# The row products of layer 4 in seven slabs: three fp16 products of split parts in place of one fp32 product

## The chip, the cores and the metric

The kernel runs on one core of a Trainium2 chip. The metric is the device time of one execution in microseconds (us). The engines have short names here: PE is TensorE (PEld its weight loads), ACT is ScalarE, DVE is VectorE, POOL is GpSimd, SP issues DMAs.

## The reference, cut to what matters

Four graph layers run one after the other over 4096 nodes with 128 features and a dense 4096 x 4096 matrix `adj`; a residual sum and a layer norm follow each. The change is in the fourth, a gated recurrent cell:

```python
def _L3_gnn_ref(states, adj, W_msg, b_msg, W_ih, W_hh, b_ih, b_hh):
    agg = adj @ states
    msg = relu(agg @ W_msg.T + b_msg)
    gi = msg @ W_ih.T + b_ih          # i_r, i_z, i_n
    gh = states @ W_hh.T + b_hh       # h_r, h_z, h_n
    r = sigmoid(i_r + h_r)
    z = sigmoid(i_z + h_z)
    n = tanh(i_n + r * h_n)
    return (1.0 - z) * n + z * states
x = layernorm(x + _L3_gnn_ref(x, adj, ...))
```

## The kernel before

**Slabs and turns.** A slab is 512 rows of `adj`, so there are eight. In layer 4 (`l == 3` in the code) PE gathers `agg` of a slab, transposed (128 features x 512 rows), in one of the two halves of the PSUM tile `acc`, slab s in half s % 2. A turn (`multiply`) is two blocks of 128 columns of `adj`. Each block takes three fp16 products of 128x512 (L629, L630, L636): both operands were split into a high and a low fp16 part, and high x high, high x low and low x high are summed. So a turn is six products, a slab has 16 turns, and layer 4 has 128. SP loads two turns' data (1 MB) at a time into six places (`group_in`), each as soon as its place is free.

**Row steps.** What follows `agg` in a slab is written as numbered steps k (`rows3` for slabs 0 to 6, `last3` for slab 7). The table `ROWS_FROM[3]` says ahead of which turn step 0 of a slab stands: 30, 43, 56, 69, 82, 96, 112 and 122 for slabs 0 to 7. PE does step k ahead of turn `ROWS_FROM + k` (`hooks`), so its row products are put between the turns. ACT and DVE hold the same steps in the same order of turns; where steps of two slabs fall on one turn, the older slab comes first. Every step waits on the count of all steps of that slab before it, in the order of the list `ROWS[3]`.

**The steps of one slab**, with PE's products in fp32 (`WT` holds the eight transposed weight matrices):

- k=0: PE transposes the slab's states into PSUM `rows_c` ("turn_h", L729).
- k=1: ACT reads `acc` into `turned` (`read_acc`, L918), and `rows_c` into `spare(own+1)` ("h_copy", L997). From then on `acc` is free for slab s+2 (`acc_reads`).
- k=3: PE, "message" (L734); k=4: ACT, relu (L1000).
- k=6, 7: PE, gates r and z, two products each (L737, L738, L741, L742); k=8: PE, "hidden_n" (L745); k=12: PE, "input_n" (L748). That is seven fp32 products in a slab.
- k=8, 10: ACT, two tanh and a bias (L1003, L1006, L1008); k=13: DVE, "r_times" and "n_in" (L1668, L1671); k=14: ACT, tanh ("n_act", L1011); k=16, 17: DVE, "h_minus_n", "z_times", "h_new" (L1674, L1677, L1680).
- k=19 to 25: PE turns the result back (L752), DVE adds x and gathers the norm's statistics, POOL takes the power, ACT scales (L949) and issues the DMA of the output.

Of the kernel before, what the change touches and what calls it, by code (L numbers as in the profile page):

```python
# [7 lines left out]
F16 = mybir.dt.float16  # L8
# [4 lines left out]
P = 128  # L13
# [28 lines left out]
Y0_LOW = 2048.0  # L42
Y_SCALE = 256.0
WHOLE = A_SCALE * Y_SCALE

# [29 lines left out]
for at, s in enumerate(ORDER[1]):  # L75
    ROWS_FROM[1][s] = ENDS1[at] if at != 1 else ENDS1[at] + 1
    if at >= 2:
# [41 lines left out]
    ["turn_h", "h_copy", "message", "message_act", "gate_r", "gate_z", "hidden_n", "r_act", "z_act", "hidden_bias",  # L119
     "input_n", "r_times", "n_in", "n_act", "h_minus_n", "z_times", "h_new", "turn_new", "combine"] + LN,  # L120
]

# [18 lines left out]
def build(nc, x, adj, w0, w1, b1, alpha, beta, w_msg, b_msg, w_ih, w_hh, b_ih, b_hh, out, scratch, dis_out):  # L141
    with ExitStack() as ctx:
# [61 lines left out]
        def kept_slot(n):  # L204
            return parts[:, 2 * UNIT * n:2 * UNIT * (n + 1)].rearrange("p (b z w) -> p b z w", z=2, w=SLAB)

        ident = sb("ident", [P, P])
        WT = sb("WT", [P, 8, P])
        bias1 = sb("bias1", [P, D])
# [15 lines left out]
        peak = sb("peak", [P, 4, 4])  # L225
        row_peak = sb("row_peak", [P, 4])
        neg_peak = sb("neg_peak", [P, 4])
        exp_sum = sb("exp_sum", [P, 4, 2])
        row_sum = sb("row_sum", [P, 2])
        inv_sum = sb("inv_sum", [P, 2])  # L230
# [28 lines left out]

        tile_in = [sem(f"tile_in{c}") for c in range(GROUPS)]  # L260
        turned_up = sem("turned_up")
        high_done = sem("high_done")
        low_done = sem("low_done")
        low_by_turns = sem("low_by_turns")
# [58 lines left out]
        def row_before(l, s, name):  # L323
            return row_base(l, s) + ROWS[l].index(name)

        acc_reads = [2, 1, 1, 1]
        acc_base = [sum(acc_reads[i] * SLABS for i in range(l)) for l in range(4)]

        def acc_reads_done(l, s):
            return acc_base[l] + (place_in(l, s) + 1) * acc_reads[l]  # L330

        def part_free(b):
            return product_base[2] + max(b - 3, 0)
# [204 lines left out]
        def _(pe):  # L538
# [170 lines left out]
            def rows2(k, s):  # L709
                if k == 8:  # L710
# [4 lines left out]
                        last = pe.transpose(acc[:, s % 2, mine], t_of[s % 2][:, q, :], ident[:])  # L715
                    last.then_inc(row[s % 2], 1)

            def rows3(k, s):
                par = s % 2
                own = 6 * par  # L720
                rows_a, rows_b, rows_c = rows_of[par]
                if k == 0:
                    pe.wait_ge(row[par], row_before(3, s, "turn_h"))
                    if s < 2:
                        pe.wait_ge(scores_read, 16 * SLABS)
                        pe.wait_ge(mixed_done, NB * SLABS)
                    pe.wait_ge(x_back[s], 16)
                    for q in range(Q):
                        last = pe.transpose(rows_c[:, P * q:P * (q + 1)], x_nat[:, Q * s + q, :], ident[:])  # L729
                    last.then_inc(row[par], 1)  # L730
                if k == 3:
                    pe.wait_ge(row[par], row_before(3, s, "message"))
                    pe.wait_ge(acc_read, acc_reads_done(3, s))
                    pe.matmul(rows_a, WT[:, 1, :], turned[par][:], start=True, stop=True).then_inc(row[par], 1)  # L734
                if k == 6:
                    pe.wait_ge(row[par], row_before(3, s, "gate_r"))
                    pe.matmul(rows_b, WT[:, 2, :], spare(own + 0), start=True, stop=False)  # L737
                    pe.matmul(rows_b, WT[:, 5, :], spare(own + 1), start=False, stop=True).then_inc(row[par], 1)  # L738
                if k == 7:
                    pe.wait_ge(row[par], row_before(3, s, "gate_z"))  # L740
                    pe.matmul(rows_c, WT[:, 3, :], spare(own + 0), start=True, stop=False)  # L741
                    pe.matmul(rows_c, WT[:, 6, :], spare(own + 1), start=False, stop=True).then_inc(row[par], 1)  # L742
                if k == 8:
                    pe.wait_ge(row[par], row_before(3, s, "hidden_n"))
                    pe.matmul(rows_a, WT[:, 7, :], spare(own + 1), start=True, stop=True).then_inc(row[par], 1)  # L745
                if k == 12:
                    pe.wait_ge(row[par], row_before(3, s, "input_n"))
                    pe.matmul(rows_b, WT[:, 4, :], spare(own + 0), start=True, stop=True).then_inc(row[par], 1)  # L748
# [91 lines left out]
        def _(act):  # L840
# [149 lines left out]
            def rows3(k, s):  # L990
                par = s % 2
                own = 6 * par
                rows_a, rows_b, rows_c = rows_of[par]
                if k == 1:
                    read_acc(3, s)
                    act.wait_ge(row[par], row_before(3, s, "h_copy"))
                    act.activation(spare(own + 1), rows_c, ACT.Copy).then_inc(row[par], 1)  # L997
                if k == 4:
                    act.wait_ge(row[par], row_before(3, s, "message_act"))
                    act.activation(spare(own + 0), rows_a, ACT.Relu, bias=gate_bias[:, 0:1]).then_inc(row[par], 1)  # L1000
                if k == 8:
                    act.wait_ge(row[par], row_before(3, s, "r_act"))
                    act.activation(spare(own + 2), rows_b, ACT.Tanh, scale=0.5, bias=half_bias[:, 0:1]).then_inc(row[par], 1)  # L1003
                if k == 10:
                    act.wait_ge(row[par], row_before(3, s, "z_act"))
                    act.activation(spare(own + 3), rows_c, ACT.Tanh, scale=0.5, bias=half_bias[:, 1:2]).then_inc(row[par], 1)  # L1006
                    act.wait_ge(row[par], row_before(3, s, "hidden_bias"))
                    act.activation(spare(own + 4), rows_a, ACT.Identity, scale=0.5, bias=half_bias[:, 2:3]).then_inc(row[par], 1)  # L1008
# [86 lines left out]
            for n in range(TURNS3):  # L1095
                if n < PAIRS // 2:
                    for k in range(3 * n, 3 * n + 3):
                        rows2(k, SLABS - 1)
                if n == 2:
                    y_high(3, SLABS - 2)  # L1100
                if n == PAIRS + 2:
                    y_high(3, SLABS - 1)
                for k, s in hooks(3, n - ACT_LEAD):
                    if s == SLABS - 1:
                        last3(k)
                    else:
                        rows3(k, s)
# [191 lines left out]
        def _(dve):  # L1299
# [74 lines left out]
            dve.tensor_scalar(scal[:, 6:7], scal[:, 4:5], -1.0 / Y_SCALE, None, ALU.mult)  # L1374
            dve.tensor_scalar(scal[:, 7:8], scal[:, 4:5], A_SCALE, None, ALU.mult)
            dve.tensor_scalar(scal[:, 5:6], scal[:, 1:2], 1.0 / XN_SCALE ** 2, None, ALU.mult)
            dve.tensor_copy(half_bias[:, 2:3], gate_bias[:, 6:7])
            link(dve.tensor_tensor(half_bias[:, 0:2], gate_bias[:, 1:3], gate_bias[:, 4:6], ALU.add))
            link(dve.tensor_scalar(half_bias[:], half_bias[:], 0.5, None, ALU.mult))
# [278 lines left out]
            def rows3(k, s):  # L1658
# [4 lines left out]

                def before(name):
                    dve.wait_ge(row[par], row_before(3, s, name))
                if k == 13:
                    before("r_times")
                    dve.scalar_tensor_tensor(spare(own + 2), spare(own + 2), 1.0, spare(own + 4), ALU.add,  # L1668
                                             ALU.mult).then_inc(row[par], 1)
                    before("n_in")  # L1670
                    dve.tensor_tensor(spare(own + 2), rows_b, spare(own + 2), ALU.add).then_inc(row[par], 1)  # L1671
# [176 lines left out]
```

## Time and profile before

| what | value |
|---|---|
| median of 3 runs | 1311.12 us (1306.46 to 1311.75) |
| the profiled execution: its time | 1309.65 us |
| the profiled execution: its span, first to last instruction | 1307.9 us |
| PE busy over the span | 1227.0 us (94%) |
| DVE, ACT, POOL busy over the span | 770.7 us (59%), 685.3 us (52%), 460.1 us (35%) |
| chain that ended last: share of PE | 78% |
| mean granted TensorE clock | 0.987 |

The time is 1.75 us above the span: what lies ahead of the first and behind the last instruction. Shares of the whole span are averages over four layers with different limits, so the part on layer 4 has to be read in layer 4's own stretch, which begins at about 1070 us; its rows steps run from 1112 us on. Matmuls are pipelined: a row's duration is longer than the distance to the next start, and it is the distance between starts that a product costs in a stream.

### The profile page before, as it was taken

The page shows a single profiled execution, that of the slowest core. Times are in us where ns is not written, and L with a number is a line of the kernel's source. Part 1 is how long each engine was busy: PE and PEld are TensorE (multiplying, and loading weights), DVE is VectorE, ACT ScalarE, POOL GpSimd, SP SyncE. Part 2 cuts the span into 40 slices and gives each one's busy share as a digit, 9 for nine tenths or more (in the row PEclk, how much of TensorE's full clock was granted, in tenths as well). Part 3 has the DMA queues.
Part 4 walks back from the last instruction along what each step waited for, and adds up shares of the span by engine and source line. Part 5 has one row for each costly group of instructions (what it writes and reads, how often), then busy time and mean ns, then how long its engine had stood idle before and what let it go on. Part 6 is the DMA issues. An engine that isn't in the chain of part 4 may idle for free.

```text
span 1307.9 us, 20934 instructions
## 1 busy us (share of the span) xinstructions
PE 1227.0 (94%) x7980; PEld 789.5 (60%) x7980; DVE 770.7 (59%) x1769; ACT 685.3 (52%) x995; POOL 460.1 (35%) x433
## 2 busy tenths in 40 slices
PE   5889999999999989869999999999999889999996
PEld 4888888887884544425555656555655544444442
DVE  6856665655643352687787878787878860122213
ACT  6555555555442222168778787878787530123222
POOL 4012231222123232325566665657565560000000
PEclk9899999999999999979999999999999999999998
DMA  9999999999978979466777777877776849978870
GB/s 304 358 416 415 406 397 377 386 350 357 352 288 320 387 299 353 177 241 247 269 265 274 258 268 267 285 268 287 269 278 213 302 178 365 390 272 315 312 267 24
DMA packets 113524, 394.20 MB, mean 301 GB/s; under 512 B 9872, under 2 KB 23440, under 8 KB 91536
## 3 DMA queue, kind: packets, MB, share of 16 engines
q1 hardware_dynamic: 105232, 388.80, 79.7%
q10 hardware_dynamic: 8192, 4.06, 1.1%
q8 instruction: 63, 1.03, 0.3%
q14 instruction: 37, 0.30, 0.1%
HBM read 319.95 MB, written 72.88 MB: 300 GB/s over the span
## 4 chain that ended last, share of the span: by engine, by line
PE 78%; DVE 8%; ACT 5%; DMA 4%; issue 4%; POOL 2%; POOLq 0%; SPq 0%; ACTq 0%; DVEq 0%
PE strip_b L688 8%; PE acc L629 6%; PE acc L630 6%; PE acc L636 6%; PE acc L707 4%; PE acc L705 4%; PE acc L704 4%; PE acc L703 4%; PE acc L605 4%; PE mid L605 4%; PE strip_b L580 3%; PE strip_a L580 3%; PE acc L603 2%; PE mid L603 2%; PE strip_a L671 2%
## 5 line engine op out<-in xcount | busy, mean ns | idle before, releaser
L1224 POOL TENSOR_TENSOR parts<-arena,parts 128x512 f16<-128x512 f32 x237 | 275.6, 1172 | 196.3 <-ACT parts L980 192.4
L980 ACT ACTIVATE parts<-arena 128x512 f16<-128x512 f32 x256 | 158.5, 624 | 111.1 <-DVE arena L1635 102.6
L1635 DVE SCALAR_TENSOR_TENSOR arena<-parts,dis,strip_b 128x512 f32<-128x512 f16 x256 | 188.9, 743 | 29.7 <-PE strip_b L688 22.5
L629 PE MATMUL acc<-arena,Y 128*128 128x512 f16 x428 | 162.8, 380 | 3.5 <-DMA arena<-adj_t 2.0
L688 PEld LDWEIGHTS strip_b<-ident,arena 128*128 128x128 f32 x1024 | 128.2, 142 | 60.9 <-DVE arena L1626 5.4
L688 PE MATMUL strip_b<-ident,arena 128*128 128x128 f32 x1024 | 155.4, 275 | 8.8 <-ACT arena L975 5.7
L630 PE MATMUL acc<-arena,Y 128*128 128x512 f16 x428 | 162.6, 380 | 0.0
L636 PE MATMUL acc<-arena,Y 128*128 128x512 f16 x428 | 162.5, 380 | 0.0
L969 ACT ACTIVATE arena<-arena,neg_peak 128x2048 f32<-128x2048 f32 x64 | 127.3, 1989 | 5.2 <-DVE neg_peak L1605 5.2
L1201 POOL TENSOR_TENSOR sc<-sc,power 128x4 f32<-128x4 f32 x31 | 31.5, 1016 | 279.6 <-DVE sc L1454 279.6
L975 ACT ACTIVATE arena<-arena,weight 128x2048 f32<-128x2048 f32 x57 | 113.4, 1989 | 2.6 <-DVE weight L1619 2.6
L1594 DVE CUSTOM_DVE_ANT_0 arena<-strip_a,arena,scal 128x1024 f32<-128x1024 f32 x64 | 82.0, 1281 | 49.8 <-PE strip_a L673 32.9
L707 PE MATMUL acc<-parts,Y 128*128 128x512 f16 x256 | 97.1, 379 | 3.4 <-POOL parts L1224 3.4
L703 PE MATMUL acc<-parts,Y 128*128 128x512 f16 x256 | 97.0, 379 | 0.1
L704 PE MATMUL acc<-parts,Y 128*128 128x512 f16 x256 | 97.0, 379 | 0.0
L705 PE MATMUL acc<-parts,Y 128*128 128x512 f16 x256 | 97.0, 379 | 0.0
L1594 DVE CUSTOM_DVE_ANT_0 arena<-mid,arena,scal 128x1024 f32<-128x1024 f32 x58 | 74.3, 1282 | 34.7 <-PE mid L673 34.7
L580 PE MATMUL strip_a<-ident,arena 128*128 128x128 f32 x512 | 67.7, 276 | 13.6 <-DVE parts L1422 10.3
L629 PEld LDWEIGHTS acc<-arena,Y 128*128 128x128 f16 x428 | 42.0, 98 | 57.4 <-issue 11.4
L630 PEld LDWEIGHTS acc<-arena,Y 128*128 128x128 f16 x428 | 42.0, 98 | 55.8 <-issue 13.1
L1668 DVE SCALAR_TENSOR_TENSOR arena<-arena 128x512 f32<-128x512 f32 x7 | 4.8, 692 | 117.4 <-PE mid L748 87.8
L605 PE MATMUL acc<-Y,parts 128*128 128x260 f16 (+1 forms) x286 | 72.8, 291 | 0.0
(332 smaller groups left out, 2559.1 us busy)
## 6 DMA issues: line engine op xcount, KB each, us to landing
arena<-adj_t SPq DMA_DIRECT2D x107, 1024.0 KB, 6.0
arena<-in_adj SPq DMA_DIRECT2D x64, 1024.0 KB, 9.5
arena<-in_adj SPq DMA_DIRECT2D x128, 512.0 KB, 5.8
parts<-adj_t SPq DMA_DIRECT2D x128, 512.0 KB, 7.3
adj_t<-parts SPq DMA_DIRECT2D x37, 1024.0 KB, 8.2
adj_t<-arena SPq DMA_DIRECT2D x27, 1024.0 KB, 9.2
scratch<-v ACTq DMA_DIRECT2D x8, 256.0 KB, 10.6
arena<-scratch SPq DMA_DIRECT2D x8, 256.0 KB, 4.6
```

Of the source, the lines that this page charges most:

```text
L605: last = pe.matmul(acc0[q][:, 0:width], high, Y[:, j, 0:width], start=False, stop=stop)
L629: pe.matmul(to, y_high, high, start=j == 2 * FIRST[l][s], stop=False)
L630: pe.matmul(to, y_low, high, start=False, stop=False)
L636: last = pe.matmul(to, y_high, low, start=False, stop=j == NB - 1)
L688: last = pe.transpose(strip_b[:, b % 2, P * q:P * (q + 1)], unit_in[:, place, P * (j % 8):P * (j % 8 + 1)], ident[:])
L703: pe.matmul(to, Y[:, j, YD:YD + D], kept_slot(b // 2 % KEPT_SLOTS)[:, b % 2, 1, :], start=j == 0, stop=False)
L704: pe.matmul(to, Y[:, j, 0:D], part_h[:, b % 4, :], start=False, stop=False)
L707: pe.matmul(to, Y[:, j, 0:D], part_l[:, b % 4, :], start=False, stop=j == NB - 1).then_inc(product, 1)
L980: act.activation(part_h[:, b % 4, :], mixed[b % G_SLOTS], ACT.Copy).then_inc(high_done, 1)
L1224: pool.tensor_tensor(part_l[:, b % 4, :], mixed[b % G_SLOTS], part_h[:, b % 4, :], ALU.subtract).then_inc(low_done, 1)
L1594: dve.tensor_tensor_reduce(unit_in[:, place, :], flat(scores_at(i)[:]), unit_in[:, place, :], scal[:, 5:6], NEG_HUGE, ALU.mult, ALU.max, p ...
L1635: dve.scalar_tensor_tensor(mixed[b % G_SLOTS], kept_slot(n % KEPT_SLOTS)[:, b % 2, 0, :], dis[:, j:j + 1], strip_b[:, b % 2, :], ALU.mult, ...
```

## The change

Every fp32 operand of the seven row products of slabs 0 to 6 is now held as a high and a low fp16 part, scaled by 16 (rows) or 256 (weights), and each product is three fp16 products. Slab 7 stays as it was. ACT writes the high part, DVE the low part (the value less its high part). The weights are split once, at the start of layer 4. `acc` is now read twice per slab (by ACT and by DVE) before it is free. The scale is undone in the ACT and DVE instructions that read the results.

```diff
+        w_high = parts[:, 12 * UNIT:12 * UNIT + 7 * P].rearrange("p (n w) -> p n w", w=P)
+        w_low = parts[:, 14 * UNIT:14 * UNIT + 7 * P].rearrange("p (n w) -> p n w", w=P)
...
-        acc_reads = [2, 1, 1, 1]
+        acc_reads = [2, 1, 1, 2]
...
+            def three(to, w, held, start, stop):
+                pe.matmul(to, w_high[:, w - 1, :], held[:, 0, :], start=start, stop=False)
+                pe.matmul(to, w_low[:, w - 1, :], held[:, 0, :], start=False, stop=False)
+                return pe.matmul(to, w_high[:, w - 1, :], held[:, 1, :], start=False, stop=stop)
...
                     pe.wait_ge(acc_read, acc_reads_done(3, s))
-                    pe.matmul(rows_a, WT[:, 1, :], turned[par][:], start=True, stop=True).then_inc(row[par], 1)
+                    if s == 0:
+                        pe.wait_ge(w_low_up, 1)
+                    three(rows_a, 1, split_row(turned[par][:]), True, True).then_inc(row[par], 1)
...
-                    pe.matmul(rows_b, WT[:, 2, :], spare(own + 0), start=True, stop=False)
-                    pe.matmul(rows_b, WT[:, 5, :], spare(own + 1), start=False, stop=True).then_inc(row[par], 1)
+                    three(rows_b, 2, split_row(spare(own + 0)), True, False)
+                    three(rows_b, 5, split_row(spare(own + 5)), False, True).then_inc(row[par], 1)
...
                 if k == 1:
-                    read_acc(3, s)
+                    act.wait_ge(product, slab_product(3, s))
+                    act.activation(split_row(turned[par][:])[:, 0, :], acc[:, par, :], ACT.Copy,
+                                   scale=ROW_SCALE / WHOLE).then_inc(acc_read, 1)
                     act.wait_ge(row[par], row_before(3, s, "h_copy"))
                     act.activation(spare(own + 1), rows_c, ACT.Copy).then_inc(row[par], 1)
+                    act.wait_ge(row[par], row_before(3, s, "h_high"))
+                    act.activation(split_row(spare(own + 5))[:, 0, :], rows_c, ACT.Copy, scale=ROW_SCALE).then_inc(row[par], 1)
                 if k == 4:
+                    act.wait_ge(row[par], row_before(3, s, "message_high"))
+                    act.activation(split_row(spare(own + 0))[:, 0, :], rows_a, ACT.Relu, scale=ROW_SCALE / ROWS3,
+                                   bias=msg_bias[:]).then_inc(row[par], 1)
                     act.wait_ge(row[par], row_before(3, s, "message_act"))
-                    act.activation(spare(own + 0), rows_a, ACT.Relu, bias=gate_bias[:, 0:1]).then_inc(row[par], 1)
+                    act.activation(spare(own + 2), rows_a, ACT.Relu, scale=ROW_SCALE / ROWS3,
+                                   bias=msg_bias[:]).then_inc(row[par], 1)
...
+                if n == 4:
+                    act.wait_ge(product, product_base[3])
+                    act.activation(w_high, WT[:, 1:8, :], ACT.Copy, scale=W_SCALE).then_inc(w_high_up, 1)
...
+                if k == 2:
+                    held = split_row(turned[par][:])
+                    dve.wait_ge(acc_read, acc_reads_done(3, s) - 1)
+                    dve.scalar_tensor_tensor(held[:, 1, :], acc[:, par, :], ROW_SCALE / WHOLE, held[:, 0, :], ALU.mult,
+                                             ALU.subtract).then_inc(acc_read, 1)
+                    before("h_low")
+                    held = split_row(spare(own + 5))
+                    dve.scalar_tensor_tensor(held[:, 1, :], rows_c, ROW_SCALE, held[:, 0, :], ALU.mult,
+                                             ALU.subtract).then_inc(row[par], 1)
+                if k == 5:
+                    before("message_low")
+                    held = split_row(spare(own + 0))
+                    dve.tensor_tensor(held[:, 1, :], spare(own + 2), held[:, 0, :], ALU.subtract).then_inc(row[par], 1)
...
+                if n == PAIRS // 2:
+                    dve.wait_ge(w_high_up, 1)
+                    dve.scalar_tensor_tensor(w_low, WT[:, 1:8, :], W_SCALE, w_high, ALU.mult,
+                                             ALU.subtract).then_inc(w_low_up, 1)
```

The other products, `z`, `hidden_n` and `input_n`, change as gate r does. "n_in" becomes one instruction that also scales.

Three places show where the new instructions stand. The first is PE at the message of slab 1 (`strip_a` is that slab's `rows_a`), before:

```order
L636 MATMUL acc<-arena,Y 128x512
L734 MATMUL strip_a<-turned,WT 128x512 [waits acc_read,row1]
L629 MATMUL acc<-arena,Y 128x512 [waits group_in5]
L630 MATMUL acc<-arena,Y 128x512
L636 MATMUL acc<-arena,Y 128x512
```

The same place in the changed kernel, where L643, L644 and L650 are the products of a turn and L733 to L735 are `three`:

```order
L650 MATMUL acc<-arena,Y 128x512
L733 MATMUL strip_a<-turned,parts 128x512 [waits acc_read,row1]
L734 MATMUL strip_a<-turned,parts 128x512
L735 MATMUL strip_a<-turned,parts 128x512
L643 MATMUL acc<-arena,Y 128x512 [waits group_in5]
L644 MATMUL acc<-arena,Y 128x512
L650 MATMUL acc<-arena,Y 128x512
```

One row became three at the same place among the turns, with the same two waits ahead of it. The second place is ACT from "n_act" of slab 0 (`row0`) to the relu of slab 1 (`row1`), before:

```order
L1011 ACTIVATE arena<-arena,gate_bias 128x512 [waits row0]
L918 ACTIVATE turned<-acc 128x512 [waits product]
L997 ACTIVATE arena<-strip_b 128x512 [waits row1]
L1000 ACTIVATE arena<-strip_a,gate_bias 128x512 [waits row1]
L1003 ACTIVATE arena<-strip_a,half_bias 128x512 [waits row1]
```

And in the changed kernel:

```order
L1043 ACTIVATE arena<-arena,gate_bias 128x512 [waits row0]
L1017 ACTIVATE turned<-acc 128x512 [waits product]
L1020 ACTIVATE arena<-strip_b 128x512 [waits row1]
L1022 ACTIVATE arena<-strip_b 128x512 [waits row1]
L1025 ACTIVATE arena<-strip_a,msg_bias 128x512 [waits row1]
L1028 ACTIVATE arena<-strip_a,msg_bias 128x512 [waits row1]
L1032 ACTIVATE arena<-strip_a,half_bias 128x512 [waits row1]
```

ACT has one instruction more ahead of the message ("h_high", L1022) and one more behind it (two relus, L1025 and L1028). The third place is DVE from "r_times" of slab 0 to its "combine", before:

```order
L1668 SCALAR_TENSOR_TENSOR arena<-arena 128x512 [waits row0]
L1671 TENSOR_TENSOR arena<-mid,arena 128x512 [waits row0]
L1674 TENSOR_TENSOR arena<-arena 128x512 [waits row0]
L1677 SCALAR_TENSOR_TENSOR arena<-arena 128x512 [waits row0]
L1680 SCALAR_TENSOR_TENSOR arena<-arena 128x512 [waits row0]
L1684 TENSOR_TENSOR t<-mid,arena 128x512 [waits row0]
```

And in the changed kernel:

```order
L1717 SCALAR_TENSOR_TENSOR arena<-arena 128x512 [waits row0]
L1720 SCALAR_TENSOR_TENSOR arena<-mid,arena 128x512 [waits row0]
L1705 SCALAR_TENSOR_TENSOR turned<-acc,turned 128x512 [waits acc_read]
L1709 SCALAR_TENSOR_TENSOR arena<-strip_b,arena 128x512 [waits row1]
L1724 TENSOR_TENSOR arena<-arena 128x512 [waits row0]
L1727 SCALAR_TENSOR_TENSOR arena<-arena 128x512 [waits row0]
L1730 SCALAR_TENSOR_TENSOR arena<-arena 128x512 [waits row0]
L1714 TENSOR_TENSOR arena<-arena 128x512 [waits row1]
L1734 TENSOR_TENSOR t<-mid,arena 128x512 [waits row0]
```

The low parts of slab 1's `agg` and states (L1705, L1709) now stand between slab 0's "n_in" and "h_minus_n", and the low part of slab 1's message (L1714) between slab 0's "h_new" and "combine".

## Rows read from the trace of the kernel before

**Rows 1.** The page's first line.

```profile
span 1307.9 us, 20934 instructions
```

**Rows 2.** Busy time by engine, granted clock, DMA share and GB/s, from 1112 us.

```profile
1112.00:1290.00 178.00, 178.00 (x750) 83.44 (x748) 37.88 (x101) 41.91 (x75) 6.06 (x6) 1.00 0.77 287
```

**Rows 3.** PE's waits from 1090 us to the end: total, times, longest.

```profile
PE strip_a L784 <- DVE arena L1720: 4.4, 1, 4.4
PE strip_a L775 <- ACT turned L918: 0.7, 1, 0.7
...
PE acc L629 <- DMA arena<-adj_t: 0.3, 1, 0.3
```

**Rows 4.** PE's timeline in slab 0's rows: start, duration, instruction.

```profile
1116.50 1.02 PE L734 MATMUL mid<-turned,WT 128*128 128x512 f32 x2
1117.36 0.38 PE L629 MATMUL acc<-arena,Y 128*128 128x512 f16 x1
...
1121.25 1.02 PE L737 MATMUL mid<-arena,WT 128*128 128x512 f32 x2
1122.11 1.02 PE L738 MATMUL mid<-arena,WT 128*128 128x512 f32 x2
1122.96 0.38 PE L629 MATMUL acc<-arena,Y 128*128 128x512 f16 x1
```

**Rows 5.** PE's groups, 1112 to 1283 us: count, busy, mean ns, idle before.

```profile
L741 PE MATMUL strip_b<-arena,WT 128*128 128x512 f32 x14 | 7.1, 592 | 0.0
```

**Rows 6.** PE's weight loads, grouped, 1112 to 1290 us.

```profile
L629 PEld LDWEIGHTS acc<-arena,Y 128*128 128x128 f16 x196 | 19.2, 98 | 26.7 <-issue 9.1
```

**Rows 7.** PE's timeline from slab 0's "input_n" to slab 1's first gate.

```profile
1133.31 1.02 PE L748 MATMUL mid<-arena,WT 128*128 128x512 f32 x2
...
1135.46 0.60 PE L729 MATMUL strip_b<-ident,arena 128*128 128x128 f32 x4
...
1139.78 1.02 PE L734 MATMUL strip_a<-turned,WT 128*128 128x512 f32 x2
...
1144.96 1.02 PE L737 MATMUL strip_a<-arena,WT 128*128 128x512 f32 x2
```

**Rows 8.** ACT's timeline in the same stretch.

```profile
1135.82 0.72 ACT L1011 ACTIVATE arena<-arena,gate_bias 128x512 f32<-128x512 f32 x1 [5.36 <-DVE arena L1671]
1136.44 0.58 ACT L918 ACTIVATE turned<-acc 128x512 f32<-128x512 f32 x1
1136.92 0.59 ACT L997 ACTIVATE arena<-strip_b 128x512 f32<-128x512 f32 x1
1140.84 0.69 ACT L1000 ACTIVATE arena<-strip_a,gate_bias 128x512 f32<-128x512 f32 x1 [3.33 <-PE strip_a L734]
```

**Rows 9.** DVE's timeline in the same stretch.

```profile
1134.37 0.69 DVE L1668 SCALAR_TENSOR_TENSOR arena<-arena 128x512 f32<-128x512 f32 x1 [54.36 <-PE mid L748]
1135.09 0.69 DVE L1671 TENSOR_TENSOR arena<-mid,arena 128x512 f32<-128x512 f32 x1
1136.57 0.69 DVE L1674 TENSOR_TENSOR arena<-arena 128x512 f32<-128x512 f32 x1 [0.79 <-ACT arena L1011]
1137.30 0.69 DVE L1677 SCALAR_TENSOR_TENSOR arena<-arena 128x512 f32<-128x512 f32 x1
1138.03 0.69 DVE L1680 SCALAR_TENSOR_TENSOR arena<-arena 128x512 f32<-128x512 f32 x1
```

**Rows 10.** Groups that split into high and low parts in other layers.

```profile
L892 ACT ACTIVATE parts<-strip_a 128x1024 f16<-128x1024 f32 x37 | 37.8, 1021 | 33.8 <-PE strip_a L580 33.8
...
L1422 DVE SCALAR_TENSOR_TENSOR parts<-strip_a,parts 128x1024 f16<-128x1024 f32 x37 | 45.2, 1221 | 23.3 <-ACT parts L892 23.3
...
L1640 DVE TENSOR_TENSOR parts<-arena,parts 128x512 f16<-128x512 f32 x19 | 16.0, 840 | 3.9 <-ACT parts L980 3.7
```

**Rows 11.** ACT's timeline at the start of layer 4.

```profile
1085.39 0.63 ACT L882 ACTIVATE Y<-arena 128x512 f16<-128x512 f32 x1 [13.66 <-DMA arena<-scratch]
```

**Rows 12.** Busy time, granted clock, DMA share and GB/s, 1100 to 1120 us.

```profile
1100.00:1120.00 20.00, 19.69 (x92) 9.01 (x91) 0.00 (x0) 1.77 (x3) 0.00 (x0) 1.00 1.01 422
```

More of the change, by code:

```diff
@@ L44 @@
 WHOLE = A_SCALE * Y_SCALE
+ROW_SCALE = 16.0
+W_SCALE = 256.0
+ROWS3 = ROW_SCALE * W_SCALE
 AHEAD = 2
@@ L118 @@
     ["x_sum", "x_scale", "turn_back", "combine"] + LN,
-    ["turn_h", "h_copy", "message", "message_act", "gate_r", "gate_z", "hidden_n", "r_act", "z_act", "hidden_bias",
+    ["turn_h", "h_copy", "h_high", "h_low", "message", "message_high", "message_act", "message_low", "gate_r", "gate_z",
+     "hidden_n", "r_act", "z_act", "hidden_bias",
      "input_n", "r_times", "n_in", "n_act", "h_minus_n", "z_times", "h_new", "turn_new", "combine"] + LN,
@@ L205, in kept_slot, with split_row @@
             return parts[:, 2 * UNIT * n:2 * UNIT * (n + 1)].rearrange("p (b z w) -> p b z w", z=2, w=SLAB)
+        w_high = parts[:, 12 * UNIT:12 * UNIT + 7 * P].rearrange("p (n w) -> p n w", w=P)
+        w_low = parts[:, 14 * UNIT:14 * UNIT + 7 * P].rearrange("p (n w) -> p n w", w=P)
+        def split_row(held):
+            return held.bitcast(F16).rearrange("p (z w) -> p z w", z=2)
         ident = sb("ident", [P, P])
@@ L227, in build @@
         neg_peak = sb("neg_peak", [P, 4])
+        msg_bias = sb("msg_bias", [P, 1])
         exp_sum = sb("exp_sum", [P, 4, 2])
@@ L261, in build @@
         turned_up = sem("turned_up")
+        w_high_up = sem("w_high_up")
+        w_low_up = sem("w_low_up")
         high_done = sem("high_done")
@@ L324, in row_before @@
             return row_base(l, s) + ROWS[l].index(name)
-        acc_reads = [2, 1, 1, 1]
+        acc_reads = [2, 1, 1, 2]
         acc_base = [sum(acc_reads[i] * SLABS for i in range(l)) for l in range(4)]
         def acc_reads_done(l, s):
-            return acc_base[l] + (place_in(l, s) + 1) * acc_reads[l]
+            return acc_base[l] + (place_in(l, s) + 1) * acc_reads[l] - (l == 3 and s == SLABS - 1)
         def part_free(b):
@@ L733, in rows3 @@
                     pe.wait_ge(acc_read, acc_reads_done(3, s))
-                    pe.matmul(rows_a, WT[:, 1, :], turned[par][:], start=True, stop=True).then_inc(row[par], 1)
+                    if s == 0:
+                        pe.wait_ge(w_low_up, 1)
+                    three(rows_a, 1, split_row(turned[par][:]), True, True).then_inc(row[par], 1)
                 if k == 6:
                     pe.wait_ge(row[par], row_before(3, s, "gate_r"))
-                    pe.matmul(rows_b, WT[:, 2, :], spare(own + 0), start=True, stop=False)
-                    pe.matmul(rows_b, WT[:, 5, :], spare(own + 1), start=False, stop=True).then_inc(row[par], 1)
+                    three(rows_b, 2, split_row(spare(own + 0)), True, False)
+                    three(rows_b, 5, split_row(spare(own + 5)), False, True).then_inc(row[par], 1)
                 if k == 7:
                     pe.wait_ge(row[par], row_before(3, s, "gate_z"))
-                    pe.matmul(rows_c, WT[:, 3, :], spare(own + 0), start=True, stop=False)
-                    pe.matmul(rows_c, WT[:, 6, :], spare(own + 1), start=False, stop=True).then_inc(row[par], 1)
+                    three(rows_c, 3, split_row(spare(own + 0)), True, False)
+                    three(rows_c, 6, split_row(spare(own + 5)), False, True).then_inc(row[par], 1)
                 if k == 8:
                     pe.wait_ge(row[par], row_before(3, s, "hidden_n"))
-                    pe.matmul(rows_a, WT[:, 7, :], spare(own + 1), start=True, stop=True).then_inc(row[par], 1)
+                    three(rows_a, 7, split_row(spare(own + 5)), True, True).then_inc(row[par], 1)
                 if k == 12:
                     pe.wait_ge(row[par], row_before(3, s, "input_n"))
-                    pe.matmul(rows_b, WT[:, 4, :], spare(own + 0), start=True, stop=True).then_inc(row[par], 1)
+                    three(rows_b, 4, split_row(spare(own + 0)), True, True).then_inc(row[par], 1)
                 if k == 19:
@@ L1001, in rows3 @@
                 if k == 8:
                     act.wait_ge(row[par], row_before(3, s, "r_act"))
-                    act.activation(spare(own + 2), rows_b, ACT.Tanh, scale=0.5, bias=half_bias[:, 0:1]).then_inc(row[par], 1)
+                    act.activation(spare(own + 2), rows_b, ACT.Tanh, scale=0.5 / ROWS3,
+                                   bias=half_bias[:, 0:1]).then_inc(row[par], 1)
                 if k == 10:
                     act.wait_ge(row[par], row_before(3, s, "z_act"))
-                    act.activation(spare(own + 3), rows_c, ACT.Tanh, scale=0.5, bias=half_bias[:, 1:2]).then_inc(row[par], 1)
+                    act.activation(spare(own + 3), rows_c, ACT.Tanh, scale=0.5 / ROWS3,
+                                   bias=half_bias[:, 1:2]).then_inc(row[par], 1)
@@ L1007, in rows3 @@
                     act.wait_ge(row[par], row_before(3, s, "hidden_bias"))
-                    act.activation(spare(own + 4), rows_a, ACT.Identity, scale=0.5, bias=half_bias[:, 2:3]).then_inc(row[par], 1)
+                    act.activation(spare(own + 4), rows_a, ACT.Identity, scale=0.5 / ROWS3,
+                                   bias=half_bias[:, 2:3]).then_inc(row[par], 1)
                 if k == 14:
@@ L1376, in _ @@
             dve.tensor_scalar(scal[:, 5:6], scal[:, 1:2], 1.0 / XN_SCALE ** 2, None, ALU.mult)
+            dve.tensor_scalar(msg_bias[:], gate_bias[:, 0:1], ROW_SCALE, None, ALU.mult)
             dve.tensor_copy(half_bias[:, 2:3], gate_bias[:, 6:7])
@@ L1670, in rows3 @@
                     before("n_in")
-                    dve.tensor_tensor(spare(own + 2), rows_b, spare(own + 2), ALU.add).then_inc(row[par], 1)
+                    dve.scalar_tensor_tensor(spare(own + 2), rows_b, 1.0 / ROWS3, spare(own + 2), ALU.mult,
+                                             ALU.add).then_inc(row[par], 1)
                 if k == 16:
```

## The prediction

> **What bounds the kernel now.** I read the span first [rows 1]: 1307.9 us, 1.75 us under the profiled execution's time of 1309.65 us. Shares over the whole span say nothing about a change in layer 4, so next come the windows from the first row step to the last turn. From 1112 to 1290 us PE is busy for all 178.00 us, at a granted clock of 1.00, which is the upper of its two levels (2.4 GHz); DVE works 37.88 us of it, ACT 41.91 us, and the DMA engines 0.77 of the time [rows 2]. Then PE's waits, for a full engine may still be one that waits in small bits: from 1090 us on there are three of note, 0.3 us for a load and, in the tail, 0.7 us and 4.4 us for ACT and DVE [rows 3]. The load's wait and the others lie outside the 178 us. So in this stretch PE's own work sets the pace: what leaves PE's stream shortens the time one for one, and work added to ACT or DVE costs nothing as long as PE never has to wait for it. The two questions are therefore the price of a product on PE, and the deadlines that the new splits have to meet.
>
> **The price of a product.** A row's duration is longer than its place in the stream, so I take distances between starts [rows 4]. The two fp32 products of gate r start at 1121.25 and 1122.11, and the next turn's product at 1122.96: 1.71 us for two, 0.855 us each. Between 1117.36 and 1121.25 stand 18 fp16 products of the same 512 columns: 3.89 / 18 = 0.216 us each. Each of these has a weight load of its own, 98 ns long [rows 6], and the pitch shows that it is hidden. Three fp16 products then take 0.648 us, and one replaced product saves 0.855 - 0.648 = 0.207 us.
>
> How many are replaced: an fp32 product leaves two records, and one line of the seven has 14 of them [rows 5], which is one product in each of seven slabs. Seven lines make 49 products (the other lines have 14 records too, some split over two banks). PE loses 49 x 0.207 = 10.1 us.
>
> **What is added beside it, and its deadlines.** The tightest place is the message of slabs 1 to 4, which stand 13 turns apart, so that ACT and DVE still finish the slab before. I follow slab 1 from the start of its transposes on PE, 1135.46, to its message, 1139.78: 4.32 us, three turns and the transposes [rows 7]. Neither moves, since no replaced product stands between them. (Slab 0's "input_n" ends 0.21 us earlier against its start, but the transposes move up with it, and so does what waits for it.)
>
> - ACT in this order: slab 0's tanh at +0.36 us, the read of `acc` at +0.98, the copy of the states from +1.46 to +2.05 [rows 8]. These stay. New behind them is "h_high", which waits on the copy's count; an instruction that waits on the one before it on its own engine starts 0.04 us after its end (1137.30 after 1136.57 + 0.69) [rows 9]. A copy of this shape takes 0.59 us [rows 8], so "h_high" ends at +2.68.
> - DVE: the low part of `agg` waits on the read of `acc` (ended at +1.56) and is done before that. "h_low" starts when "h_high" has ended, and takes 0.69 us like the other 512-column instructions [rows 9]: it ends at +3.41. With 0.05 us to PE the message could start at +3.46. It is wanted at +4.32: 0.86 us to spare.
> - The bounds of these two instructions are the same split in layer 1: at twice the width 1021 ns on ACT and 1221 ns on DVE [rows 10], so at least half of that, 0.51 and 0.61. Upwards I take the relu with its bias from memory, 0.69 us [rows 8], and the slowest subtraction of high parts, 840 ns [rows 10]. With both upper ends the message could start at +3.71, still 0.6 us early. In the middle I keep 0.59 and 0.69, since those rows have the very shape.
>
> The message's own split comes next. ACT's relu starts 1.06 us after the start of the message on PE (1140.84 against 1139.78), that is 0.205 us after its place in the stream; with the shorter product it starts at 0.85 us, and ends at 1.54. The second relu ends at 2.27 us, DVE's subtraction at 3.0 us (3.15 us with 840 ns). Ahead of it in DVE's queue are "h_minus_n", "z_times" and "h_new" of slab 0, now behind "h_low": three times 0.73 us from +3.41, so free at +5.6, which is 1.3 us after the message's start. The first gate is wanted 5.18 us after the message's start now and 4.97 us then [rows 7]: 1.8 us or more to spare. "h_new" itself, late by 1.6 us behind "h_low" [rows 9], is wanted by the transposes just ahead of that gate, more than 3 us later.
>
> `acc` is held longer: slab 2 takes over slab 0's half two turns and the transposes (about 3.0 us) after slab 0's row steps begin; ACT sees PE's end 0.2 us later and reads for 0.58 us, so DVE's read starts by +0.9 and ends by +1.8 us (840 ns). The other slabs have five turns or more.
>
> The split of the weights (896 columns, about 1 us on each engine by the rows of twice this width) stands where ACT is idle for 13.66 us [rows 11] and DVE for 54.36 us [rows 9], and its result is wanted 40 us later. All this costs nothing. Were the cover gone, a wait of x at the message would come back once a slab: 7x in all.
>
> **What could take the gain back.** The loads must keep up with a faster PE. In this stretch they move 287 GB/s [rows 2]; the same bytes in 168 us are 304 GB/s, and the queue has shown 422 GB/s [rows 12]. Only the first 20 us are close: the loads are still catching up there, at full rate, after the 0.3 us wait [rows 3]. PE takes 1 MB in 12 products, 2.59 us, or 405 GB/s, which is under 422, and every row product only widens this. I take nothing off.
>
> The tail, 1290 us to the end, belongs to slab 7, whose products are unchanged, and moves up as a whole.
>
> **Sum.** 1309.65 - 10.1 = 1299.5 us for an execution like the profiled one. That one lies 1.5 us under the median of the runs shown; from the median it would be 1301.0 us. I say 1300 us.
>
> **Rivals.**
>
> *The message waits for its split (7 in 100).* If hand-overs between ACT and DVE take longer than these rows show, PE waits at the message, in seven slabs. It starts to cost when "h_low" is 0.86 us later than worked out. At 1.6 us later half the gain is gone (7 x 0.73 = 5.1 us): 1304.6 us. For it: two instructions on two engines now stand one behind the other in a window that was just long enough for one copy and its margin. Against it: each row in the chain has been seen at its length, and upper ends leave 0.6 us.
>
> *The weight loads of the fp16 products are not hidden (3 in 100).* This ends on the other side. There are 147 fp16 products, and 98 ns each [rows 6] would add 14.4 us: 1309.65 - 10.1 + 14.4 = 1313.9 us, slower than before. It decides from 69 ns on (10.1 / 147), that is, when two thirds of a load show. Against it stands the pitch of 0.216 us in a stream whose stationary operand changes with each product [rows 4]; for it only that the new weights lie in another buffer. The Trainium skill speaks for this rival: "TensorE: Matmul & The Clock Gate", in Part 3 under what overlaps and what doesn't, says that a weight load overlaps matmuls in flight only when its row group differs, and these loads take all rows. By that rule the sum would be 1313.9 us; this trace doesn't agree, with 98 ns of load inside 216 ns of pitch.
>
> *The loads become the bound (5 in 100).* In the first turns PE's gain would turn into a wait for DMA. At most slab 0's part is lost, 7 x 0.207 = 1.4 us: 1301 us. The DMA share of 0.77 speaks against more.
>
> *Something else of PE's order costs as much as it saves (3 in 100):* about 1310 us. No row speaks for it.
>
> **How the numbers follow.** The forecast has 82 in 100. A measurement of this kernel can tell about 0.5%, 6.6 us, from no change. The forecast and the loads as bound lie beyond it (87 in 100); the late message (5.1 us gained), the visible weight loads (4.3 us lost) and part of the last case lie within it (11); 2 are left for slower. The range begins under the lowest run shown less the saving (1306.46 - 10.1 = 1296.4), at 1295.5, and reaches up to the late message, at 1305.
>
> **What the changed profile would show.** Right: 49 threes of fp16 products whose starts are 0.216 us apart, and 0.65 us from the first to the turn's next product; PE busy without a gap from slab 0's rows to the last turn, about 168 us; "h_low" ended 0.6 to 0.9 us ahead of the message of slabs 1 to 4; a span near 1297.8 us. Wrong: PE's waits list the message behind DVE's writing of the states or the gates behind the message's low part; starts of the fp16 threes more than 0.25 us apart; waits for loads after 1112 us; or a granted clock under 1.00 in this stretch.

## The result and the profile after

The changed kernel took 1299.01 us (median of 4 runs, 1297.1 to 1299.96) against 1309.95 us of the kernel before in the same runs (1306.46 to 1311.75). The ratio on record is 0.9922 (the two medians alone give 0.9916), with a 95% interval of 0.9908 to 0.9936: 8.4 to 12.1 us faster. The forecast was 1300 us.

The page of the changed kernel begins with its span:

```profile
span 1296.8 us, 21070 instructions
```

It is 11.1 us shorter than [rows 1]. Not all of this is the change. ACT's first read of `acc` in layer 4 came at 1112.38 us before and at 1111.83 us after, 0.55 us earlier, though ahead of it only the split of the weights was added, in idle time; the ten profiled executions of this study put that read between 1110.0 and 1114.3 us. So the stretch from this read (slab 0) to the same read of slab 7 is the better measure of layer 4. ACT's timeline shows the two reads before:

```profile
1112.38 0.60 ACT L918 ACTIVATE turned<-acc 128x512 f32<-128x512 f32 x1 [26.36 <-PE acc L636]
...
1290.05 0.60 ACT L918 ACTIVATE turned<-acc 128x512 f32<-128x512 f32 x1 [4.91 <-PE acc L636]
```

And after:

```profile
1111.83 0.60 ACT L1017 ACTIVATE turned<-acc 128x512 f16<-128x512 f32 x1 [26.23 <-PE acc L650]
...
1279.16 0.60 ACT L939 ACTIVATE turned<-acc 128x512 f32<-128x512 f32 x1 [4.91 <-PE acc L650]
```

That is 177.67 us before and 1279.16 - 1111.83 = 167.33 us after, 10.34 us less. The tail behind it hardly changed, 17.85 and 17.64 us.

Busy time by engine, granted clock, DMA share and GB/s of that stretch, and PE's waits from 1080 us to the end (total, times, longest), of the changed kernel:

```profile
1112.00:1280.00 168.00, 167.31 (x797) 79.30 (x795) 51.84 (x122) 51.32 (x90) 6.43 (x6) 1.00 0.80 302
```

```profile
PE strip_a L805 <- DVE arena L1770: 4.4, 1, 4.4
PE acc L643 <- DMA arena<-adj_t: 1.8, 2, 1.4
PE strip_a L796 <- ACT turned L939: 0.7, 1, 0.7
PE strip_a L799 <- ACT arena L1067: 0.3, 1, 0.3
```

Against [rows 2], DVE works 14 us and ACT 9 us more in a shorter stretch, and still no wait of PE for a row step has appeared: the waits for ACT and DVE are those of the tail, as in [rows 3], and those for loads lie at 1087 and 1101 us, ahead of the first row step. (The 0.7 us that PE isn't busy in the window is the tail's wait, which begins at 1279 us.)

PE's timeline around the two products of gate r in slab 0 (start, duration, instruction) answers to [rows 4]:

```profile
1120.27 0.38 PE L650 MATMUL acc<-arena,Y 128*128 128x512 f16 x1
1120.49 0.38 PE L733 MATMUL mid<-arena,parts 128*128 128x512 f16 x1
1120.70 0.38 PE L734 MATMUL mid<-arena,parts 128*128 128x512 f16 x1
1120.92 0.38 PE L735 MATMUL mid<-arena,parts 128*128 128x512 f16 x1
1121.13 0.38 PE L733 MATMUL mid<-arena,parts 128*128 128x512 f16 x1
1121.35 0.38 PE L734 MATMUL mid<-arena,parts 128*128 128x512 f16 x1
1121.57 0.38 PE L735 MATMUL mid<-arena,parts 128*128 128x512 f16 x1
1121.78 0.38 PE L643 MATMUL acc<-arena,Y 128*128 128x512 f16 x1
```

Six products from 1120.49 to 1121.78 take 1.29 us, 0.215 us each, where two fp32 products took 1.71 us. Each of the six has a weight load of its own. This row shows it for one of their three lines, and the other two lines have the same count and length (min/median/max in ns):

```profile
L735 PEld LDWEIGHTS mid<-arena,parts x16: 98/98/98, 1120.7 to 1270.8; 128*128 128x128 f16 x16
```

The chain that the prediction called the tightest, slab 1 from its transposes to its message, of PE, ACT and DVE in turn:

```profile
1133.44 0.60 PE L748 MATMUL strip_b<-ident,arena 128*128 128x128 f32 x4
...
1137.76 0.38 PE L733 MATMUL strip_a<-turned,parts 128*128 128x512 f16 x1
...
1142.73 0.38 PE L733 MATMUL strip_a<-arena,parts 128*128 128x512 f16 x1
```

```profile
1134.90 0.59 ACT L1020 ACTIVATE arena<-strip_b 128x512 f32<-128x512 f32 x1
1135.52 0.60 ACT L1022 ACTIVATE arena<-strip_b 128x512 f16<-128x512 f32 x1
1138.61 0.69 ACT L1025 ACTIVATE arena<-strip_a,msg_bias 128x512 f16<-128x512 f32 x1 [2.49 <-PE strip_a L735]
1139.33 0.69 ACT L1028 ACTIVATE arena<-strip_a,msg_bias 128x512 f32<-128x512 f32 x1
```

```profile
1136.15 0.69 DVE L1709 SCALAR_TENSOR_TENSOR arena<-strip_b,arena 128x512 f16<-128x512 f32 x1 [0.42 <-ACT arena L1022]
...
1140.05 0.69 DVE L1714 TENSOR_TENSOR arena<-arena 128x512 f16<-128x512 f32 x1 [1.15 <-ACT arena L1028]
```

The low part of the states is done at 1136.84, 3.40 us after the transposes began; the message is wanted at 4.32 us. With 0.05 us to PE that leaves 0.87 us. The message's own low part is done 2.98 us after the message's start, and the first gate starts 4.97 us after it.

### The profile page after: what moved, and what is told of

It reads as the page before. It is cut to its first block, busy times and chain, and to the rows that moved or that the text cites. A ratio compares the mean times of both kernels' runs of the same rounds, so it can differ in the third digit from the quotient of the medians.

```text
span 1296.8 us, 21070 instructions
## 1 busy us (share of the span) xinstructions
PE 1217.1 (94%) x8029; PEld 787.2 (61%) x8029; DVE 786.5 (61%) x1792; ACT 695.1 (54%) x1010; POOL 460.0 (35%) x433
## 4 chain that ended last, share of the span: by engine, by line
PE 80%; DVE 7%; ACT 4%; issue 4%; DMA 3%; POOL 2%; POOLq 0%; SPq 0%; ACTq 0%; DVEq 0%
PE strip_b L702 8%; PE acc L643 6%; PE acc L650 6%; PE acc L644 6%; PE acc L721 4%; PE acc L718 4%; PE acc L719 4%; PE acc L717 4%; PE acc L619 4%; PE mid L619 4%; PE strip_b L594 4%; PE strip_a L594 3%; PE acc L617 2%; PE mid L617 2%; PE strip_a L685 2%
## 5 line engine op out<-in xcount | busy, mean ns | idle before, releaser
L643 PE MATMUL acc<-arena,Y 128*128 128x512 f16 x428 | 162.3, 379 | 3.2 <-DMA arena<-adj_t 1.8
L650 PE MATMUL acc<-arena,Y 128*128 128x512 f16 x428 | 162.2, 379 | 0.0
L644 PE MATMUL acc<-arena,Y 128*128 128x512 f16 x428 | 162.2, 379 | 0.0
L1630 DVE CUSTOM_DVE_ANT_0 arena<-mid,arena,scal 128x1024 f32<-128x1024 f32 x58 | 74.4, 1283 | 34.7 <-PE mid L687 34.7
L643 PEld LDWEIGHTS acc<-arena,Y 128*128 128x128 f16 x428 | 41.9, 98 | 52.5 <-DMA arena<-adj_t 4.0
L619 PE MATMUL mid<-Y,parts 128*128 128x260 f16 (+1 forms) x286 | 73.0, 292 | 0.0
L650 PEld LDWEIGHTS acc<-arena,Y 128*128 128x128 f16 x428 | 41.9, 98 | 49.6
## 6 DMA issues: line engine op xcount, KB each, us to landing
scratch<-v ACTq DMA_DIRECT2D x8, 256.0 KB, 10.9
```

Source lines behind the costliest of these rows:

```text
L619: last = pe.matmul(acc0[q][:, 0:width], high, Y[:, j, 0:width], start=False, stop=stop)
L643: pe.matmul(to, y_high, high, start=j == 2 * FIRST[l][s], stop=False)
L644: pe.matmul(to, y_low, high, start=False, stop=False)
L650: last = pe.matmul(to, y_high, low, start=False, stop=j == NB - 1)
L1630: dve.tensor_tensor_reduce(unit_in[:, place, :], flat(scores_at(i)[:]), unit_in[:, place, :], scal[:, 5:6], NEG_HUGE, ALU.mult, ALU.max, p ...
```

## The experiments

The theory: PE's stream alone sets the pace of this stretch, so the gain is the difference between a fp32 product and three fp16 ones, 49 times; everything added to ACT and DVE is free until the margin of 0.87 us at the message is used up. Its rivals: the splits cost something that the products more than paid for; the gain came from something that goes with fp32, such as its weight loads or its records, and not from the length of the products; the loads become the bound; a late message costs less, or more, than its wait. Eight kernels were run. The table has the measured medians beside the stretch in each profile (the two reads of `acc` by ACT, slab 0 and slab 7). Each ratio is taken against executions of the kernel before that were run beside that kernel, with medians of 1309.95 us (the changed kernel), 1308.99 us (split parts beside fp32, four, two, one) and 1308.57 us (the last four rows), so it isn't a quotient of this column.

| kernel | median, us | ratio to before, 95% interval | stretch, us | against the change, us |
|---|---|---|---|---|
| before | 1309.95 | 1 | 177.67 | +10.34 |
| changed | 1299.01 | 0.9922 (0.9908 to 0.9936) | 167.33 | 0 |
| fp32 products, all splits beside | 1308.84 | 1.0002 (0.9994 to 1.0011) | 177.66 | +10.33 |
| four fp16 products | 1309.32 | 1.0005 (0.9996 to 1.0015) | 177.91 | +10.58 |
| two | 1288.2 | 0.9848 (0.9835 to 0.9862) | 156.75 | -10.58 |
| one | 1276.23 | 0.9758 (0.9744 to 0.9771) | 146.18 | -21.15 |
| one, without making low parts | 1278.22 | 0.9767 (0.9751 to 0.9783) | 146.18 | -21.15 |
| late by one instruction | 1298.6 | 0.9924 (0.9906 to 0.9941) | 167.33 | 0.00 |
| late by three | 1301.9 | 0.9947 (0.993 to 0.9965) | 171.44 | +4.11 |
| late by five | 1313.1 | 1.0033 (1.0021 to 1.0046) | 182.94 | +15.61 |

### The splits alone, on the kernel before

```diff
                     act.activation(spare(own + 1), rows_c, ACT.Copy).then_inc(row[par], 1)
+                    act.wait_ge(row[par], row_before(3, s, "h_high"))
+                    act.activation(split_row(spare(own + 5))[:, 0, :], rows_c, ACT.Copy, scale=ROW_SCALE).then_inc(row[par], 1)
...
+                    before("message_low")
+                    dve.tensor_tensor(beside(par)[:, 1, :], spare(own + 0), beside(par)[:, 0, :],
+                                      ALU.subtract).then_inc(row[par], 1)
```

The other splits stand where the change has them.

> The kernel before with its fp32 row products, and all the splits of the change beside them: the same added ACT and DVE instructions at the same places, the same added waits, the second read of the accumulator, the split of the weights; nothing reads the split parts. Theory (PE's stream alone sets the pace, the splits meet their deadlines): the same as before, 1310 us within 1.5 us, and no PE wait for ACT or DVE between 1112 us and the last turn. Rival (the splits cost something on the path, and the products gave more than they lost): 1311.5 us or more, with waits of PE at the message or the gates.

The ratio is 1.0002, and the stretch is 177.66 us against 177.67 us. Of PE's waits from 1112 us to slab 7's read there is none. The splits cost nothing where PE's products leave them room, and the rival falls.

### Four, two and one fp16 product

```diff
                 pe.matmul(to, w_low[:, w - 1, :], held[:, 0, :], start=False, stop=False)
+                pe.matmul(to, w_low[:, w - 1, :], held[:, 1, :], start=False, stop=False)
                 return pe.matmul(to, w_high[:, w - 1, :], held[:, 1, :], start=False, stop=stop)
```

> The changed kernel with a fourth fp16 product (low weights by low rows) in each of the 49 places. Theory (an fp16 product costs 0.216 us wherever it stands, and an fp32 product is worth four of them): 49 x 0.216 = 10.6 us slower than the change, 1309.6 us, the time of before within 1.5 us. Rival (the gain came from something other than the number of passes, such as the fp32 weight loads or the fp32 records): part of the gain stays, 1307 us or less.

```diff
                 pe.matmul(to, w_high[:, w - 1, :], held[:, 0, :], start=start, stop=False)
-                pe.matmul(to, w_low[:, w - 1, :], held[:, 0, :], start=False, stop=False)
                 return pe.matmul(to, w_high[:, w - 1, :], held[:, 1, :], start=False, stop=stop)
```

> The changed kernel without the product of the low weights (leaves out the low part of the weights, so it computes with rounded weights). Theory: 49 x 0.216 = 10.6 us less than the change, 1288.4 us within 2 us, ratio to before 0.983 to 0.985; the loads are asked for 325 GB/s in the stretch and still keep up. Rival (the loads become the bound, or the next deadline is missed): 1292 us or more, with PE waiting for loads, or for ACT or DVE, in the stretch.

```diff
-                pe.matmul(to, w_high[:, w - 1, :], held[:, 0, :], start=start, stop=False)
-                pe.matmul(to, w_low[:, w - 1, :], held[:, 0, :], start=False, stop=False)
-                return pe.matmul(to, w_high[:, w - 1, :], held[:, 1, :], start=False, stop=stop)
+                return pe.matmul(to, w_high[:, w - 1, :], held[:, 0, :], start=start, stop=stop)
```

> The changed kernel with only the product of the high parts (leaves out the low parts of rows and weights; they are still computed). Theory: 98 x 0.216 = 21.2 us less than the change, 1277.8 us within 3 us; the loads are asked for some 347 GB/s over the stretch and 405 GB/s between the row products, under the 422 GB/s seen. Rival (the loads become the bound): 1283 us or more with PE waits for loads spread over the stretch.

Each product more or less moves the stretch by 10.58 us, 49 x 0.216 us, up and down alike (21.15 / 98 = 0.216 for two). Four fp16 products take 0.24 us more over the whole stretch than the fp32 product, so one fp32 product costs what four fp16 ones do, less 5 ns, 0.859 us. The fourth product gives back the whole gain, so nothing of it is left for a cause beside the length of the products. How the engine fills the 0.859 us of an fp32 product no run here shows. PE's timeline of the kernel with four shows them at one product of gate r:

```profile
1120.54 0.38 PE L733 MATMUL mid<-arena,parts 128*128 128x512 f16 x1
1120.75 0.38 PE L734 MATMUL mid<-arena,parts 128*128 128x512 f16 x1
1120.97 0.38 PE L735 MATMUL mid<-arena,parts 128*128 128x512 f16 x1
1121.18 0.38 PE L736 MATMUL mid<-arena,parts 128*128 128x512 f16 x1
1121.40 0.38 PE L733 MATMUL mid<-arena,parts 128*128 128x512 f16 x1
```

The rival with the loads was put hardest by one product. Busy time, clock, DMA share and GB/s of that kernel from 1112 us to just ahead of slab 7's read:

```profile
1112.00:1256.00 144.00, 144.00 (x689) 68.66 (x686) 50.99 (x121) 49.19 (x86) 6.42 (x6) 1.00 0.88 347
```

PE is busy throughout at 347 GB/s of loads, and waits for none of them. So the loads weren't near to being the bound at the change's 302 GB/s.

### One product, without the instructions that make low parts

```diff
-                if k == 2:
-                    held = split_row(turned[par][:])
-                    dve.wait_ge(acc_read, acc_reads_done(3, s) - 1)
...
-                if k == 5:
-                    before("message_low")
```

> One fp16 product in each of the 49 places (leaves out the low parts of rows and weights) without the instructions that made the low parts: two DVE instructions for rows, one for the message, the second relu, the second read of the accumulator and the weights' low part are gone. Theory (these instructions lie beside PE's stream): the time of the kernel with one product and all splits, 1276 us within 1.5 us. Rival (they cost something): 1274 us or less.

Both stretches are 146.18 us: 21 DVE instructions for rows and seven relus on ACT less change nothing. The medians differ by 2 us the other way (1278.22 against 1276.23 us), so the time expected, 1276 us within 1.5 us, was missed by 0.7 us. The intervals of the two ratios overlap, and in the profiled executions the difference lies ahead of the stretch, in the place of slab 0's read, 1112.24 and 1110.12 us. For the medians the same cause is likely but not shown.

### The message made late

```diff
                     held = split_row(spare(own + 5))
+                    for n in range(3):
+                        dve.scalar_tensor_tensor(parts[:, SLAB * n:SLAB * (n + 1)], rows_c, ROW_SCALE, held[:, 0, :], ALU.mult,
+                                                 ALU.subtract)
                     dve.scalar_tensor_tensor(held[:, 1, :], rows_c, ROW_SCALE, held[:, 0, :], ALU.mult,
                                              ALU.subtract).then_inc(row[par], 1)
```

> The changed kernel with one useless DVE instruction of the same form ahead of the low part of the states in each slab, 0.61 us more on the message's split. Theory (the message has 0.87 us to spare in slabs 1 to 4, 1.6 us and more in the others): the time of the change, 1299 us within 1.5 us, ratio to before 0.991 to 0.994. Rival (the margin is thinner than the trace says, or DVE's queue behind it is late): up to 7 x 0.61 = 4.3 us slower.

> The same with three useless instructions, 1.83 us more. Theory: PE waits 0.96 us at the message of slabs 1 to 4 and 0.2 us in slabs 0 and 5, 4.2 us in all: 1303.2 us within 1.5 us. Rival (a PE wait is hidden by something later, or costs a fall of the granted clock): 1299 us, or 1305 us and more with the granted clock under 1.00 in the stretch.

> The same with five useless instructions, 3.05 us more: past the point at which the late message eats up the gain. Theory: PE waits 2.18 us at the message of slabs 1 to 4, 1.4 us in slabs 0 and 5, 1.0 us in slab 6, 12.5 us in all: 1311.5 us within 2 us, no faster than before. Rival (other waits join, or the granted clock falls in these gaps): 1315 us or more.

One instruction, 0.61 us, left the stretch at 167.33 us to the hundredth. Three, which by the trace made the low part of the states 1.80 us late, brought waits just where the margin said (1.80 - 0.87 = 0.93 us). PE's waits of that kernel in the stretch, and its message of slab 1:

```profile
PE mid L733 <- DVE arena L1712: 1.5, 2, 0.8
PE strip_a L733 <- DVE arena L1712: 1.5, 2, 0.8
```

```profile
1137.02 0.39 PE L733 MATMUL strip_a<-turned,parts 128*128 128x512 f16 x1 [0.77 <-DVE arena L1712]
```

Four waits of 0.77 us are the four slabs that stand 13 turns apart. A matmul is drawn 0.38 us long and takes 0.216 us of the stream, so a wait is really 0.16 us longer than it is shown: 4 x 0.93 = 3.7 us, and with the small delays of slabs 0 and 5 the 4.11 us of the stretch; 4.2 us were expected.

Five, 3.00 us late by the trace, went past the point where the gain is gone, as expected. The median of 1313.1 us even lies within the 2 us of the theory, but the stretch grew by 15.61 us and not by 12.5 us. The waits shown sum to 11.0 us in seven slabs, 12.1 us with 0.16 us for each. The rest is the clock. PE's timeline at slab 1's message, and the windows around the messages of slabs 1 and 2 (the number behind the engines is the granted clock):

```profile
1141.09 0.48 PE L733 MATMUL strip_a<-turned,parts 128*128 128x512 f16 x1 [1.96 <-DVE arena L1712]
1141.37 0.63 PE L734 MATMUL strip_a<-turned,parts 128*128 128x512 f16 x1
1141.80 0.63 PE L735 MATMUL strip_a<-turned,parts 128*128 128x512 f16 x1
```

```profile
1138.00:1141.00 3.00, 1.13 (x6) 0.29 (x3) 3.00 (x7) 0.00 (x0) 0.00 (x0) 1.00 0.96 360
1141.00:1144.00 3.00, 2.91 (x8) 1.06 (x9) 2.11 (x5) 1.37 (x2) 0.00 (x0) 0.54 0.75 309
1144.00:1147.00 3.00, 3.00 (x14) 1.30 (x13) 0.60 (x1) 0.00 (x0) 0.00 (x0) 0.89 0.00 0
...
1164.00:1167.00 3.00, 1.19 (x6) 0.34 (x4) 3.00 (x6) 0.00 (x0) 0.00 (x0) 1.00 0.94 366
1167.00:1170.00 3.00, 2.84 (x14) 1.31 (x15) 2.63 (x5) 1.37 (x2) 0.00 (x0) 1.00 0.33 139
```

In the 3 us behind slab 1's wait the granted clock is 0.54, near the lower of its two levels (1.2 GHz), and the products start 0.43 us apart; behind the equally long wait of slab 2 it stays at 1.00. At slab 3's message the clock fell again (0.74 from 1191 to 1194 us and 0.69 from there to 1197 us), at slab 4's it did not. ACT's reads of `acc` in slabs 1 to 4 give the price:

```profile
1135.63 0.58 ACT L1017 ACTIVATE turned<-acc 128x512 f16<-128x512 f32 x1
...
1161.69 0.58 ACT L1017 ACTIVATE turned<-acc 128x512 f16<-128x512 f32 x1
...
1186.07 0.58 ACT L1017 ACTIVATE turned<-acc 128x512 f16<-128x512 f32 x1
...
1212.14 0.58 ACT L1017 ACTIVATE turned<-acc 128x512 f16<-128x512 f32 x1
```

From read to read it is 26.06 us over slab 1's message, 24.38 us over slab 2's and 26.07 us over slab 3's, so a fall costs about 1.7 us here, and two of them 3.4 us: 12.1 + 3.4 = 15.5 us. So of the two theories on this run the wait was right in size, and the rival was right that the clock would add to it, though by less than the 1315 us or more that it gave.

## Why the prediction was right

**What bounds the stretch.** Shown: with PE's own work changed by a product more, one less and two less, the time followed one for one, and with ACT's and DVE's work changed alone (splits beside fp32 products, low parts left out, one instruction more) it didn't move.

**The price of a product.** Predicted 0.207 us saved per product and 10.1 us in all; the stretch lost 10.34 us, 0.211 us each. The count of 49 and the fp16 price of 0.216 us were right. The fp32 price was read as 0.855 us from two starts given to the hundredth; it is 0.859 us. The remaining 0.6 us of the 10.9 us between the medians lies outside the stretch, within the scatter of the other layers. That the median came within 1 us of the forecast is in part luck, since the place of the first row step alone differs by up to 4.3 us between executions; the 10.34 us are what bears the prediction out.

**The deadlines.** "h_low" was to allow the message at +3.46 us, and allowed it at +3.45 us; the message's low part at 3.0 us, and it came at 2.98 us; the gate at 4.97 us, as it did. The spare 0.86 us at the message was 0.87 us by the trace, and the run with 0.61 us more showed no wait while the one with 1.80 us more did. The second read of `acc` in slab 0 ended 1.52 us after the transposes began, under the 1.8 us allowed, and the split of the weights took 0.93 us on ACT and 1.08 us on DVE in idle time. Two slips in the prediction's working changed nothing. By its own terms "h_new" ends at +5.60 us instead of the +3.26 us of [rows 9], which is 2.3 us late and not 1.6 us; the trace has it 2.2 us late, and still 3.4 us ahead of the transposes that want it. And the rows from which the split of 896 columns was sized are 1024 columns wide, not twice its width.

**The loads.** 304 GB/s were worked out and 302 GB/s measured; no wait in the stretch.

**The rivals.** The late message didn't occur. Where it was made to occur, the waits set in between 0.61 and 1.80 us of delay, as the margin of 0.86 us says, but the price of 7x was wrong in its terms. It gives all seven slabs the margin of the tightest four; slabs 0, 5 and 6 have more. At 1.80 us of delay 7x is 6.6 us, and the stretch grew by 4.11 us. At 3.00 us 7x is 15.0 us, near the 15.61 us measured, but by luck: the waits came to 12.1 us, and the clock, which the price left out, fell twice and made up the difference. The weight loads stay hidden: 98 ns of load inside 0.215 us of pitch, with all rows loaded each time. On this the rule that was cited from the Trainium skill ("TensorE: Matmul & The Clock Gate", Part 3, what overlaps and what doesn't) doesn't agree with the measurement, and the measurement decides. The Trainium skill, in Part 2 of the same page under back-to-back issue gap, gives N / 2.4 + 2.5 ns for N columns on a warm clock, about 216 ns for 512, and the 0.216 us here agree. The Trainium skill calls this, in the same place, the gap of an isolated product and gives about 131 ns for a sustained stream of loads and products; the stream here, at 0.216 us, doesn't agree with that, and the measurement decides.

## What to carry to other kernels

In a stretch where one engine has no gap, price an edit by the distance between the starts of that engine's instructions, not by their durations: a product of 512 columns is drawn 0.38 us long and costs 0.216 us. For all that is added to other engines, find the one deadline that is nearest and count the margin; here it was right to a few hundredths. To price a missed deadline, count the margin of each slab by itself. Where the accuracy allows fewer parts, leaving one of the three fp16 products out in all 49 places is worth another 10.6 us; the kernels with two products and with one, which round the weights or both operands of these products to fp16, beat both the kernel before and the changed one.

## What the runs showed that was not expected

The rival of the last run had named a fall of the clock, but not its size or that it comes and goes. Behind a PE wait drawn as 1.96 us, in an otherwise gapless stream, the granted clock fell in two slabs of four (0.54 against 1.00 in the 3 us behind slabs 1 and 2), at a price of about 1.7 us, nearly that of the wait itself; behind waits of 0.77 and 1.20 us, in this run and the one with three, it stayed at 1.00. What decides between the slabs stays open. And the start of layer 4's row steps differed by up to 4.3 us between profiled executions whose work ahead of it was the same but for the split of the weights, while the stretch behind it repeated to 0.01 us where PE's products were the same. No run shows where ahead of it the time differs. A difference of 1% in such a kernel is better read in its own stretch than in the whole time.
